# Expert blocks of a two-layer transformer with a mixture of experts, loaded as 128-byte pieces and turned by VectorE instead of TensorE

## What is computed

```
xn = layernorm(x)
x  = x + attention0(xn) + ffn0(xn)        # ffn0: top 1 of 8 experts, relu, biases
xn = layernorm(x)
x  = x + attention1(xn) + ffn1(xn)        # ffn1: shared expert + top 2 of 8, silu, gates by softmax

expert e:   y = act(x @ w1[e].T) @ w2[e].T        # 128 -> 512 -> 128
```

## Time and profile before

| what | us |
|---|---|
| median of 3 runs | 1690.1 (1683.86 to 1692.0) |
| the profiled execution | 1683.17 |
| its span | 1681.4 |
| TensorE busy | 1416.9 (84%) |
| VectorE busy | 1098.2 (65%) |
| GpSimd busy | 1063.9 (63%) |
| ScalarE busy | 924.6 (55%) |
| DMA engines, share of the span | 25.2% queue q1 (SyncE), 5.2% q0 (GpSimd), 1.8% q10 (ScalarE) |
| mean granted share of TensorE's clock | 0.923 |

### The profile page before, as it was taken

The page is one execution under the profiler, slowest core; times in us unless marked ns, Lnnn a source line. Parts: engine busy times, 40 slices in busy tenths (PEclk is TensorE's granted clock), DMA queues, the critical chain, the costliest instruction groups (busy, mean ns, idle before and its releaser), DMA issues. The chain is left out here.

```text
span 1681.4 us, 41351 instructions
## 1 busy us (share of the span) xinstructions
PE 1416.9 (84%) x14738; PEld 1089.8 (65%) x14739; DVE 1098.2 (65%) x1833; ACT 924.6 (55%) x1565; POOL 1063.9 (63%) x827
## 2 busy tenths in 40 slices
PE   7849999999999999997199958887978579999970
PEld 5535666666666666664199956765656479999970
DVE  5558999999999999995365634643724323333329
ACT  7718888888888888885044425522323234444430
POOL 7614888888888888889344435535776734444440
PEclk9959999999999999998599978988989889999995
DMA  7962333333333333310633334200111112222228
GB/s 228 304 188 63 82 86 89 88 86 87 87 87 83 83 85 83 84 28 16 187 89 100 89 110 156 65 29 32 40 41 39 43 57 66 67 65 66 63 57 295
DMA packets 113324, 155.15 MB, mean 92 GB/s; under 512 B 18080, under 2 KB 84896, under 8 KB 108576
## 3 DMA queue, kind: packets, MB, share of 16 engines
q1 hardware_dynamic: 88352, 115.03, 25.2%
q0 software_dynamic: 13600, 28.45, 5.2%
q10 hardware_dynamic: 11232, 9.73, 1.8%
HBM read 95.33 MB, written 57.82 MB: 91 GB/s over the span
## 5 line engine op out<-in xcount | busy, mean ns | idle before, releaser
L871 ACT ACTIVATE Ex<-pB 128x512 f32<-128x512 f32 x512 | 524.4, 1104 | 108.4 <-PE pB L682 105.1
L912 POOL TENSOR_TENSOR V<-Ex,R 128x4096 f32<-128x4096 f32 x64 | 479.9, 7498 | 76.1 <-DVE R L793 76.1
L771 DVE TENSOR_REDUCE mg<-pA 128x128 f32<-128x2048 f32 x128 | 289.5, 2261 | 14.7 <-PE pA L665 11.8
L787 DVE TENSOR_REDUCE Z<-Ex 128x64 f32<-128x2048 f32 x128 | 290.8, 2274 | 5.4 <-ACT Ex L871 5.2
L682 PEld LDWEIGHTS pB<-qk 72*128 72x128 bf16 x2048 | 157.9, 97 | 122.7 <-issue 1.6
L1066 POOL DMA_INDIRECT y_d<-x1yb,x1xb x136 | 130.6, 960 | 152.9 <-DVE x1yb L1181 81.3
L677 PE MATMUL pB<-mh,identb 128*128 128x512 bf16 x512 | 198.1, 387 | 14.7 <-ACT Ex L871 2.4
L682 PE MATMUL pB<-qk 72*128 72x128 bf16 x2048 | 199.0, 219 | 0.0
L677 PE MATMUL pB<-ml,identb 128*128 128x512 bf16 x512 | 194.3, 379 | 0.0
L692 PE MATMUL pO<-V,Vh 128*8 128x128 f32 x4096 | 161.1, 278 | 12.0 <-POOL V L912 12.0
L1693 POOL DMA_INDIRECT xs_d<-d_xn,d_idx x128 | 127.9, 1000 | 41.8 <-issue 40.1
(11 more groups left out here) (250 smaller groups left out, 2295.9 us busy)
## 6 DMA issues: line engine op xcount, KB each, us to landing
qk<-qs_d SPq DMA_DIRECT2D x96, 192.0 KB
qk<-ks_d SPq DMA_DIRECT2D x96, 192.0 KB
x1xb<-xs_d SPq DMA_DIRECT2D x136, 64.5 KB
f_ye<-y_d SPq DMA_DIRECT2D x16, 512.0 KB, 4.3
qs_d<-parts SPq DMA_DIRECT2D x16, 384.0 KB, 3.0
ks_d<-parts SPq DMA_DIRECT2D x16, 384.0 KB, 3.1
x0xb<-xs_d SPq DMA_DIRECT2D x72, 64.5 KB
xn_d<-xn SPq DMA_DIRECT2D x16, 258.0 KB, 3.3
```

Source lines behind the costliest of these rows:

```text
L771: dve.tensor_reduce(mg[:, :, g], pA[:].rearrange("p b q -> p q b"), AX.X, ALU.max).then_inc(b_red, 1)
L787: dve.tensor_reduce(Z[:, q], Ex[:, j, q, :], AX.X, ALU.add).then_inc(b_sum, 1)
L871: act.activation(Ex[:, j, :, BG * g:BG * (g + 1)].rearrange("p q b -> p b q"), pB[:, g % 2, :, :], ACT.Exp).then_inc(b_exp, 1)
L912: pool.tensor_tensor(En[:, j % 2, :, :].rearrange("p b q -> p q b"), Ex[:, j, :, :], R[:, j % 2, :].unsqueeze(2).broadcast_to([P, P, B]), ...
```

## The change

The block is no longer loaded as it lies. A block is 128 tokens by 128 features; cut into 4 by 4 squares of 32 by 32, `load_part` brings feature square b of all four token squares to partitions 32b to 32b+31, so that token t of square a lies in partition 32b+t at place 32a. Each of its four DMAs moves 128 pieces of 32 words (128 bytes). With every square then turned in itself by one VectorE instruction (`turn_x`), the block stands with features on partitions, as `up` wants it. The pieces b = 0 and 1 are issued by SyncE, 2 and 3 by ScalarE (`load_x`, six blocks ahead, AHEAD). The tag is loaded by a DMA of its own, 128 pieces of 4 bytes, issued by SyncE four blocks later (LATER) than that block's pieces. Pieces wait only until the block that was in the slot has been turned (`e_xT`); tags wait for the scatter as before. TensorE's transposes, their PSUM tiles and ScalarE's copies are gone. SyncE now reads the starts of twelve blocks at once, once in eight blocks; ScalarE reads each block's start by itself. GpSimd waits for the tag as well.

```diff
 P = 128
+SQ = 32
 B, S, D = 32, 256, 128
...
 RND = 8
+AHEAD = 6
+LATER = 4
 NB0 = -(-(NS + E - 1) // RND) * RND
...
         e_x = [sem(f"e_x{i}") for i in range(RND)]
-        e_xp = sem("e_xp")
+        e_t = [sem(f"e_t{i}") for i in range(RND)]
         e_xT = sem("e_xT")
...
             with ExitStack() as ph:
-                xb = sb(pre + "xb", [P, RND, DR], F32, ph)
+                xb = sb(pre + "xb", [P, RND, D], F32, ph)
+                tag = sb(pre + "tag", [P, RND, 1], F32, ph)
                 xT = sb(pre + "xT", [P, 2, P], F32, ph)
...
                 yb = sb(pre + "yb", [P, RND, D], F32, ph)
-                pX = [pb(f"{pre}pX{i}", [P, P], ph) for i in range(2)]
                 pU = [pb(f"{pre}pU{i}", [P, 2, HID], ph) for i in range(2)]
...
+                def load_part(eng, q, rows, b):
+                    eng.dma_start(xb[b * SQ:(b + 1) * SQ, q, :].rearrange("t (a d) -> t a d", d=SQ),
+                                  rows[:, b * SQ:(b + 1) * SQ].rearrange("(a t) d -> t a d", t=SQ))\
+                       .then_inc(e_x[q], 16)
                 loads = [0]
...
                 def _(sp):
-                    def body(k, q):
-                        first = sp.value_load(bs[0:1, bass.ds(k, 1)], min_val=0, max_val=E * REG + (SPARE - 1) * P)
+                    def starts_of(k):
+                        loads[0] += 1
+                        n = RND + LATER if started(k, RND) else RND
+                        regs = [sp.alloc_register(f"{pre}s{loads[0]}_{j}") for j in range(n)]
+                        sp.load(regs, bs[0:1, bass.ds(k + RND - n, n)])
+                        return [None] * (RND + LATER - n) + \
+                            [sp.snap(reg, donate=True, min_val=0, max_val=E * REG + (SPARE - 1) * P) for reg in regs]
+                    def load_tag(k, q, first):
                         if started(k, RND):
...
                             settle(sp, settled)
-                        sp.dma_start(xb[:, q, :], xs[bass.ds(first, P), :]).then_inc(e_x[q], 16)
+                        sp.dma_start(tag[:, q, :], xs[bass.ds(first, P), D:DR],
+                                     allow_slow_non_contiguous=True).then_inc(e_t[q], 16)
+                    def body(k, q):
+                        if q == 0:
+                            firsts[:] = starts_of(k)
+                        if started(k, RND):
+                            sp.wait_ge(e_xT, k0 + k - RND + 1)
+                            settle(sp, settled)
+                        for b in range(2):
+                            load_part(sp, q, xs[bass.ds(firsts[q + LATER], P), :], b)
+                        if started(k, LATER):
+                            load_tag(k - LATER, (q - LATER) % RND, firsts[q])
                         if layer == 0 and q == 0 and not beyond(k, 8, nb):
...
                                          w2_1[:, bass.ds(k * (HID // RND), HID)]).then_inc(c_w1, 16)
+                    firsts = [None] * (RND + LATER)
                     rounds(sp, nb, body, RND)
+                    for k in range(nb - LATER, nb):
+                        load_tag(k, k % RND, firsts[RND + LATER - nb + k])
...
                         pool.wait_ge(e_yb, k0 + k + 1)
+                        pool.wait_ge(e_t[q], 16 // RND * (k0 + k - q) + 16)
                         settle(pool, settled)
                         pool.indirect_dma_start(
-                            out=y, out_offset=bass.IndirectOffsetOnAxis(xb[:, q, D:DR].bitcast(U32), 0),
+                            out=y, out_offset=bass.IndirectOffsetOnAxis(tag[:, q, :].bitcast(U32), 0),
                             in_=yb[:, q, :], in_offset=None).then_inc(e_st[q], 16)
...
                 def _(pe):
-                    def transpose_x(k, q):
-                        pe.wait_ge(e_x[q], 16 // RND * (k0 + k - q) + 16)
-                        if started(k, 2):
-                            pe.wait_ge(e_xT, k0 + k - 1)
-                        nc.tensor.transpose(pX[q % 2][:], xb[:, q, 0:D], ident[:]).then_inc(e_xp, 1)
                     def up(k, q):
...
                             es[:] = experts_of(pe, k)
-                        if not beyond(k, 2, nb):
-                            transpose_x(k + 2, (q + 2) % RND)
                         if not beyond(k, 1, nb):
...
                     pe.wait_ge(w_in, 32 * E)
-                    transpose_x(0, 0)
-                    transpose_x(1, 1)
                     up(0, 0)
...
                 def _(act):
-                    def copy_x(k, q):
-                        act.wait_ge(e_xp, k0 + k + 1)
-                        if started(k, 2):
-                            act.wait_ge(e_u, k0 + k - 1)
-                        act.copy(xT[:, q % 2, :], pX[q % 2][:]).then_inc(e_xT, 1)
+                    def load_x(k, q):
+                        first = act.value_load(bs[0:1, bass.ds(k, 1)], min_val=0, max_val=E * REG + (SPARE - 1) * P)
+                        if started(k, RND):
+                            act.wait_ge(e_xT, k0 + k - RND + 1)
+                            settle(act, settled)
+                        for b in range(2, 4):
+                            load_part(act, q, xs[bass.ds(first, P), :], b)
...
                             es[:] = experts_of(act, k)
-                        if not beyond(k, 2, nb):
-                            copy_x(k + 2, (q + 2) % RND)
+                        if not beyond(k, AHEAD, nb):
+                            load_x(k + AHEAD, (q + AHEAD) % RND)
                         if not beyond(k, 1, nb):
...
                     es = [None] * (RND + 3) if layer == 1 else experts_of(act, 0)
-                    copy_x(0, 0)
-                    copy_x(1, 1)
+                    for k in range(AHEAD):
+                        load_x(k, k)
                     leave_up(0, 0, es[0])
...
                 def _(dve):
+                    def turn_x(k, q):
+                        dve.wait_ge(e_x[q], 64 // RND * (k0 + k - q) + 64)
+                        if started(k, 2):
+                            dve.wait_ge(e_u, k0 + k - 1)
+                        dve.transpose(xT[:, q % 2, :], xb[:, q, :]).then_inc(e_xT, 1)
                     def stage_w(k, q, e):
...
                             leave_up(k + 1, (q + 1) % RND, es[q + 1])
+                        if not beyond(k, 2, nb):
+                            turn_x(k + 2, (q + 2) % RND)
                         finish(k, q, es[q])
...
                         stage_w(k, k, es[k])
+                    turn_x(0, 0)
+                    turn_x(1, 1)
                     if layer == 0:
```

## The result

The changed kernel took **1711.2 us** (median of 4 runs, 1703.4 to 1716.3) against 1687.8 of the kernel before on the same chip: a ratio of 1.0158, 95% interval 1.0112 to 1.0204. Times are medians; the ratios are estimated from the fast executions alone and are not exactly the quotients of the medians (three executions of the experiments were slower than their fellows by over 1.5%). The profiled execution took 1707.7 us with a span of 1705.9, 24.5 more than before. As a change of the profiled execution, 35.0 us were forecast and 24.5 measured.

What follows compares the result with a forecast made beforehand. TensorE bounded the kernel before; ScalarE's queue was to bound the changed one. Layer 1's 6.1, layer 0's 22.0 and the starts' 3.8 and 3.1 made 35.0 us more than 1683.2, 1718.2; forecast 1720, range 1688 to 1752.

Steps and rivals of the forecast that it cites:

- Part 1: TensorE in both expert phases loses 208 transposes of 0.11 us, 22.9 us, if nothing else becomes later.
- Part 2, layer 1: ScalarE's queue gets a register load and two DMA issues: 2.02 us a block, 6.1 us more in layer 1.
- under 1.9 us apart: Sign that the forecast is wrong: ACTIVATEs follow each other under 1.9 us apart.
- The bound worked out for 1.86 a block: Lower bound for ScalarE's queue: layer 1 goes by TensorE and the turn's wait, 2 below now; total 1700.
- the turn's place: Rival: at 1.8 to 1.95 us on ScalarE, waits for VectorE's turn replace the transposes' gain; about 1685, chance 0.18.
- Part 2, layer 0: ScalarE's queue needs 2.17 us a block plus register loads of expert numbers: 22.0 us more in layer 0.
- Part 3: Start of each phase: ScalarE issues six blocks' loads before the first leave_up; 3.8 us more in layer 1, 3.1 in layer 0.
- Part 4: VectorE's turn takes 0.3 us; its waits stay hidden while ScalarE's block lasts over 2.0, else cost about 13 and 5 us.
- Part 5: SyncE's queue needs some 1.95 us a block, 2.09 in layer 0, nearly as full as ScalarE's; GpSimd's extra wait costs nothing.
- Part 6: Small transfers take 0.59 us of every DMA engine a block, at most 1.37; priced at nothing, hidden by the queues' 2.02.
- TensorE gave nothing measurable back: Rival: TensorE stays the bound if ScalarE's queue needs under 1.8 us a block; 1667, chance 0.15.
- SyncE's queue was, at 0.06: Rival: SyncE's queue is the bound if issues take 0.45, at 2.25 and 2.39 us a block; 1743 and more, chance 0.06.

Runs made afterwards that it cites:

- the runs with relieved queues: Changed kernel with starts read once a round, turn early, lead four: 1669.3 us with SyncE loading whole rows, 1678.5 us with tags shared with ScalarE.
- The early turn: Changed kernel with four turned inputs, VectorE turning block k+3 ahead of leave_up instead of k+2 behind it: 1693.3 us, ratio 1.0126.

## Why the prediction was right, and where it was not

The sign and the range held, and in layer 0, where most of the loss is, the main cause was the forecast one: ScalarE's queue became the bound. The sum was 35.0 us; its four terms as measured make 28.0, and the execution's 24.5 are lower still by a shorter stretch between the phases, which is luck and no part of the forecast.

- **Part 1, TensorE's transposes, 22.9 us.** They went, and nearly none of it arrived: 0.2 us a round in layer 1. What TensorE could have given shows in the runs with relieved queues: rounds of 15.3 in place of 16.0, 10 us over layer 1. At 0.11 a block it would have been 15.
- **Part 2, layer 1: the term that was mis-sized.** Priced 2.02 us a block; measured 1.85 by its parts and 1.88 from ACTIVATE to ACTIVATE. Too much were the load with its DMA (1.26, taken from SyncE, against 1.20), the second issue (0.54 against 0.49 to 0.50), and 0.07 for a value worked out for the wait, which happens once a round. So layer 1 rose by 0.7 and not by 6.1, and "under 1.9 us apart", my own sign of an error, came true. The path was wrong as well. TensorE was to wait for ScalarE at `down` in every block; it waited there for 2.7 us in the whole layer, and the wait came once a round before `up`, behind its queue's load of expert numbers. The bound worked out for 1.86 a block, with layer 1 at 2 below now, came within 3 us of layer 1, but by luck: it had TensorE's own pace right and charged the rest to the turn's place, and with the turn moved the rounds stayed at 15.8.
- **Part 2, layer 0: 22.0 priced, 20.5 measured.** The queue needs 2.05 and not 2.17 a block, but its load of expert numbers lasted 1.22 to 1.34 and not 1.20. The early turn showed the queue's round alone: 18.3 where the kernel has 18.6.
- **Part 3, the starts: 3.8 and 3.1 priced, 3.7 and 3.1 measured.** The cut to four blocks gave back 3.2 and 2.6.
- **Part 4, VectorE's turn.** 0.30 us held, and so did the 1.05 from the end of an `up` to the next one, to the hundredth. That this is hidden did not hold in layer 0: I set the 1.05 against the 0.90 of `down` and so took the loop for less than the queue's block. It is `up`'s whole 1.16 to its last product, and then the 1.05: 2.21, above the queue's 2.05. The early turn took 5.6 us off layer 0 by that. The Trainium skill (VectorE: DVE Perf Modes, the three transpose paths) has 311 ns for bf16; the fp32 turn took 302 ns in layer 0 and 305 in layer 1 (medians), close to the page's figure for the other type.
- **Part 5, SyncE.** Its queue did not bind in the changed kernel, and "nearly as full" was right; that a small shift makes it the bound (17.1 a round) was not foreseen, and comes from GpSimd's scatters, which I had costed on GpSimd alone.
- **Part 6, the transfers.** 0.161 of 16 engines over 261 us and 55016 packets are 12.2 ns a packet on SyncE's queue (its 4-byte tags among them), 13.7 ns on ScalarE's, in place of 30.4 ns before; 0.57 us of every engine a block, where 0.59 was priced. The Trainium skill (DMA: Bandwidth & Descriptors, specifications) wants 512 bytes for line rate and has less read, modified and written; from that I concluded that a piece would be dearer than a row, which the page does not say. Here a packet cost less than half. By the byte it cost more, as the page's line rate has it: 4.27 MB took 12.3% of the engines where 8.54 MB had taken 13.6%. Whole rows of 512 bytes in place of the pieces changed nothing measurable.

The rivals: TensorE gave nothing measurable back in either layer, though in layer 1 15.3 of the 15.8 us a round are its own. The turn's place was real in layer 0, as a second bound on top of the first and not in its stead. SyncE's queue was, at 0.06, the one that I took too lightly; it took over in four of the experiments.

## What to carry to other kernels

Count an engine's queue like an engine: a DMA with a start from a register cost 0.50 us of the issuing queue here, and its register load with the check and the wait 0.70 more, whatever the engine's busy time says. Before moving work from the busiest engine to others, add up the queue of each for a round; here three queues and one loop stood within 10% of each other, so a relief alone gained nothing or 6 us, where all of them together gained 10 to 11 us in layer 1 and 15 to 22 in layer 0. Then place the change only in the phase whose queues have room; here that was worth 0.3%, at the edge of what was measured.

## What the runs showed of the hardware

- **A GpSimd scatter holds up SyncE's queue.** With scatters a 29 ns move took up to 708 ns, ending about 1.3 us after the scatter's start; without them none did, and rounds of 17.1 us became 15.9. ScalarE's moves were not touched in those 100 us, and one of 264 was over the layer.
- **What a register load costs depends on where it begins as well as on its length.** On ScalarE's queue: one value 0.28 us, eight from k+4 0.55, ten from k+4 0.99, eight from k+6 1.80 (k a multiple of eight). Only these cases were measured.
- **On the queues of 128-byte pieces from HBM a packet cost 12 to 14 ns of a DMA engine on average**, closing packets and tags among them, where on the queue of 516-byte rows it cost 30.
- **What a register load on TensorE's queue costs depends on when it starts.** The load of eleven expert numbers lasts 1.3 to 1.4 us; started 1.01 us before the last product ended, it left TensorE idle for 0.76, and started 0.42 before, for 1.29.
